# Turning by products in column groups, and loads, reciprocals and first value products moved by some slots, in a one-core attention and FFN layer

## The reference

```python
def _L0_attn_ref(x, Wq, Wk, Wv, Wo, bo):
    q = (x @ Wq).reshape(B, C, H, D).transpose(0, 2, 1, 3)   # k and v alike
    scores = jnp.einsum('bhqd,bhkd->bhqk', q, k)
    scores = jnp.where(causal, scores, -jnp.inf)
    attn = jax.nn.softmax(scores / jnp.sqrt(jnp.float32(E)), axis=-1)
    ctx = jnp.einsum('bhqk,bhkd->bhqd', attn, v)
    return ctx.transpose(0, 2, 1, 3).reshape(B, C, E) @ Wo + bo
...
def _L0_ffn_ref(x, weight, bias):
    xq, xs = _mx_quantize(x2)      # blocks of 32, nearest value of a 6-bit grid
    wq, ws = _mx_quantize(w2)
    return (xq * xs) @ (wq * ws).T + bias
...
x = x + _L0_attn_ref(_layernorm(x), ...)
x = x + _L0_ffn_ref(_layernorm(x), ...)
```

## Time and profile before

| what | value |
|---|---|
| median of 3 runs | 2030.56 us (2029.66 to 2031.16) |
| the profiled execution | 2027.43 us |
| its span, first to last instruction | 2025.7 us |
| mean granted TensorE clock | 0.978 of full speed |
| busy: PE, DVE, ACT, POOL | 93%, 84%, 66%, 40% |

### The profile page before, as it was taken

How to read it: one execution, slowest core, us unless ns; L and a number is a source line. 1 busy time by engine, 2 the same in 40 slices (tenths; PEclk the granted TensorE clock), 3 DMA queues, 4 the chain that set the end, 5 groups by cost and what they waited for, 6 DMA issues and landing times.

```text
span 2025.7 us, 72471 instructions
## 1 busy us (share of the span) xinstructions
PE 1878.4 (93%) x30309; PEld 823.9 (41%) x30309; DVE 1706.3 (84%) x4358; ACT 1342.0 (66%) x2817; POOL 811.1 (40%) x1123
## 2 busy tenths in 40 slices
PE   6799899898999999999999999999999999999994
PEld 2334344343344343534334344434443444444432
DVE  4798897878997979797898979797799899999975
ACT  5357666676776767676676766667666676777660
POOL 4323324231344545454243646444345444211232
PEclk9899999999999999999999999999999999999987
DMA  5442231413132251612414161340613221140000
GB/s 161 124 105 83 60 88 37 116 53 96 41 95 76 72 125 44 142 53 64 114 47 117 38 158 54 79 111 19 161 49 88 68 71 51 39 100 27 11 33 22
DMA packets 173349, 156.51 MB, mean 77 GB/s; under 512 B 43224, under 2 KB 160734, under 8 KB 173022
## 3 DMA queue, kind: packets, MB, share of 16 engines
q1 hardware_dynamic: 173020, 151.88, 27.9%
HBM read 91.89 MB, written 57.02 MB: 74 GB/s over the span
## 4 chain that ended last, share of the span: by engine, by line
PE 56%; DVE 27%; SPq 6%; issue 5%; ACT 3%; POOL 2%; DMA 2%; POOLq 0%; DVEq 0%; ACTq 0%
PE psum L1459 39%; PE psum L1500 15%; DVE max_parts L1202 12%; DVE psum L1197 7%; SPq L677 5%; ACT probs L1015 2%; DVE max_parts L1197 1%; PE psum L1527 1%; ACT acc_sb L1024 1%; PE psum L1519 1%; DVE block_max L1331 1%; DMA qk_scratch<-shop 1%; DVE out_shop L1354 1%; DVE out_shop L1362 1%; DVE stats L1290 1%
## 5 line engine op out<-in xcount | busy, mean ns | idle before, releaser
L1015 ACT ACTIVATE probs<-psum 128x512 f32<-128x512 f32 (+3 forms) x2560 | 1209.9, 538 | 461.3 <-PE psum L1459 448.1
L1202 DVE TENSOR_REDUCE max_parts<-psum 128x1 f32<-128x512 f32 x1536 | 960.1, 682 | 97.8 <-PE psum L1459 93.5
L1459 PE MATMUL psum<-k_rows,q_rows 96*32 96x512 bf16 (+3 forms) x10240 | 851.6, 352 | 65.2 <-DVE max_parts L1197 31.8
L1459 PE MATMUL psum<-q_rows,k_rows 99*32 99x512 bf16 (+3 forms) x10240 | 892.6, 351 | 9.2 <-DMA q_rows<-max_rows 3.9
L1500 PE MATMUL psum<-probs,v_in 128*17 128x512 f32 (+3 forms) x5120 | 591.3, 535 | 15.8 <-ACT acc_sb L1024 15.1
L1197 DVE CUSTOM_DVE_ANT_0 psum<-psum,causal 128x128 f32<-128x128 f32 (+3 forms) x1024 | 475.4, 518 | 97.6 <-PE psum L1459 93.7
L1459 PEld LDWEIGHTS psum<-k_rows,q_rows 96*32 96x32 bf16 x10240 | 280.0, 97 | 475.1 <-DVE max_parts L1202 162.8
L1459 PEld LDWEIGHTS psum<-q_rows,k_rows 99*32 99x32 bf16 x10240 | 282.9, 96 | 402.0 <-ACT probs L1015 209.7
L843 POOL TENSOR_SCALAR_AFFINE_SELECT probs<-probs 128x512 f32<-128x512 f32 x256 | 165.2, 645 | 652.2 <-ACT probs L1015 651.9
L1500 PEld LDWEIGHTS psum<-probs,v_in 128*17 128x17 f32 x5120 | 143.0, 98 | 111.4 <-issue 33.9
L1197 DVE DVE_READ_ACCUMULATOR2_ANT max_parts<- 128x1 f32 x1024 | 145.1, 142 | 0.0
(11 more groups left out here) (157 smaller groups left out, 1205.2 us busy)
## 6 DMA issues: line engine op xcount, KB each, us to landing
q_rows<-qk_scratch SPq DMA_DIRECT2D x384, 64.0 KB, 2.7
k_rows<-qk_scratch SPq DMA_DIRECT2D x384, 64.0 KB, 2.6
qk_scratch<-shop SPq DMA_DIRECT2D x56, 384.0 KB, 3.4
sums_scratch<-acc_sb SPq DMA_DIRECT2D x48, 256.0 KB, 2.3
shop<-in_L_attn_x SPq DMA_DIRECT2D x19, 512.0 KB, 4.4
v_scratch<-shop SPq DMA_DIRECT2D x16, 544.0 KB, 4.3
v_in<-v_scratch SPq DMA_DIRECT2D x64, 136.0 KB, 2.9
out_shop<-in_L_attn_x SPq DMA_DIRECT2D x12, 512.0 KB, 8.7
```

The lines of the kernel that those rows point to most:

```text
L1015: nc.scalar.activation(probs[s % NPROBS][:, h, a:CHUNK], bank[SCORE_BANKS[n % 3]][:, a:CHUNK], ACT.Exp, scale=SCALE).then_inc(probs_ready, 1)
L1202: nc.vector.tensor_reduce(max_parts[k % 2][:, first:first + heads, t % TILES, c], ring_bank(UNIT_USE[n])[:, 0:heads * width] .rearrange("p ...
L1459: ins = nc.tensor.matmul(out[r:r + COLUMNS], weights[:, r:r + COLUMNS], moving, start=start, stop=stop)
```

## The change

Four edits. The load of x of chunks 4 to 15 is placed at start - 6 in place of start - 2, four slots earlier in SP's order. `invert` is placed from p + 7 on in place of p + 5, two slots later, and by that the output work of a chunk behind it, by 2 to 7 slots for most. The turns are made by `by_columns`, as products of the block with the unit matrix: 16 products of 32 columns for four blocks, in place of 4 transposes of 128 columns (`turn_weights`, once, stays). And the first `values` of each row chunk stands after h = 3 in place of h = 1.

```diff
 def place_project(n, start):
-    sync(start - 2, "load_x", n)
+    sync(start - 6, "load_x", n)
...
-            p = vector(p + 5, 0.6, "invert", n) + 1
+            p = vector(p + 7, 0.6, "invert", n) + 1
...
             def turn_acc(k):
...
-                    ins = nc.tensor.transpose(ring_bank(use)[:, j * P:(j + 1) * P], acc_sb[k % 2][:, j * P:(j + 1) * P],
-                                              ident[:, :])
+                    ins = by_columns(ring_bank(use)[:, j * P:(j + 1) * P], acc_sb[k % 2][:, j * P:(j + 1) * P],
+                                     ident[:, :], True, True)
...
             def turn_x(n, e):
...
-                    ins = nc.tensor.transpose(ring_bank(use)[:, j * P:(j + 1) * P],
-                                              x_in[n % 2][:, j, e * P:(e + 1) * P], ident[:, :])
+                    ins = by_columns(ring_bank(use)[:, j * P:(j + 1) * P], x_in[n % 2][:, j, e * P:(e + 1) * P],
+                                     ident[:, :], True, True)
...
-                    if h == 1 and 0 <= p - 2 < NS:
+
+                    if 0 <= p - 2 < NS and h == (3 if p - 2 in FIRSTS else 1):
                         values(p - 2)
```

4 lines of the change are left out of this document (2 added, 2 removed).

## The result

The changed kernel is slower. Its median is 2045.62 us (2042.77 to 2048.05, 4 runs) beside 2030.11 us of the kernel before on the same chip, a ratio of 1.0078 with an interval of 1.0064 to 1.0091: +15.5 us, where the forecast was -6.1 and the range ended at 2038. The profiled execution took 2047.51 us with a span of 2045.8, 20.1 us over the 2025.7 of before.

What follows compares the result with a forecast made beforehand. TensorE, busy 93% of the span, was taken to bound the kernel. Stalls -18.3, clock -7.8, prologue +4.7, turns +19.3 and first values -4 gave -6.1 us: 2024.5 us, range 2012 to 2038.

Steps and rivals of the forecast that it cites:

- The four stalls: TensorE's stalls behind VectorE's loads of x and denominators go, -18.3 us, and their half-clock windows, -7.8 us.
- The prologue: Chunk 4's earlier load of x delays load_rows(0, 2), so PE stands longer in slot 0: +4.7 us.
- The turns: Turns as two-pass products, 0.109 us a pass: +15 us in the slots, +2.3 prologue, +2.0 tail, in all +19.3.
- rival of dear turns: Weight loads of the turn products don't hide, 0.138 us a pass: +18 us, 2042 us; chance 0.13.
- factor of four: Turn products lose the fast float32 transpose mode, 1.74 us for four blocks, some 2095 us; one part in a hundred within dear turns.
- The first failed step: Output work behind the later invert finds other free places, none in the tail: 0, with 3 us on both sides.
- the stalls move: Rival: something else late takes the place of the loads, half of the 26 us stays: +13, 2037 us; chance 0.12.
- the term of the first values: In slots with first values, the 15.1 us wait mostly returns as another: -4 us, ends -15 and +3.
- the reciprocals: invert two slots later removes three stalls at the denominators' loads, 13.0 - 0.5 us, and 5.3 us of half clock.
- the load of x: Four slots earlier, chunk 7's stall goes, 5.75 us and 2.5 us of half clock, against +4.7 us in the prologue.
- rival of cheap turns: VectorE's lag hides half the turns' cost, most of the values' 15.1 us wait goes: -19, 2011 us; chance 0.17.
- PE has no stall over 2 us between 130 and 1900 us: Sign of the forecast: after the change TensorE has no stall over 2 us in that stretch.

Runs made afterwards that it cites:

- hand_moves: Kernel before, load of x of chunk 7 and reciprocals with their loads for chunks 0, 4, 8 moved after planning: 2014.79 us beside 2029.36.
- units_behind: Kernel before with first values after the fourth score group and the units of h = 2 and 3 behind them: 2038.28 us beside 2030.67.
- values_only: Kernel before with only the first values of each row chunk after h = 3 in place of h = 1: 2037.51 us beside 2029.9.

## Why the forecast was wrong

**The four stalls (-18.3, clock -7.8)** were read rightly, in place, cause and size. All four went, with their windows at 1.2 GHz; in hand_moves the four places give 24.5 us together, against 26.1 of the sum.

**The prologue (+4.7)** was right for the edit alone. The wait for `k_rows` near 95 us was to grow from 0.7 to about 5; in the kernel with that edit alone it is 4.6 us near 98, and slot 20 is 4.7 us later. In the changed kernel slot 0 begins 3.7 us later than before already, and the wait is 2.3 us, until 100.17.

**The turns (+19.3)** were right in the price of a pass (0.109 us, from the earlier trace rows) and in the count. The term measured 15.2 us as a median and 18.4 between spans. The rival of dear turns, with 0.138 us a pass, is out. Its small chance for a factor of four can be settled too. Four blocks take 0.87 us as products and 0.59 as transposes up to the next group, so the factor here is 1.5; against 0.44 us, the 0.68 of the earlier trace rows without the 0.24 that go with the change of mode, it is 2. The Trainium skill, TensorE: Matmul & The Clock Gate, Terms, calls the transpose mode four times faster for float32; these products in column groups don't bear that out. The Trainium skill, TensorEngine Tiling (Array Packing), Key Properties, says that a change of the tiling mode drains the TensorE; the rows agree, with 0.24 us for a turn of four.

**The first failed step** is the sentence "The output work behind goes 2 to 7 slots later into other free places, and none of it into the tail: I take 0, with 3 us on both sides." In the kernel with that edit alone 6.3 and 10.1 us are lost at two places, some 5 and 10 of them by waits and half clock. What was missed is two steps off: the output work takes free places that projections had, the projections' store moves by three slots, and in SP's order it falls behind a block of twelve loads that takes 6.7 us to issue. GpSimd waits for that store, with a mask in its queue that TensorE needs. The forecast looked at SP's order at the prologue and at chunk 7, and not at the stores whose slots moved. The rival that came nearest is "the stalls move", 2037 us; it named another statistics step or the first store of the inverse, not this one. The edit gave 4.3 us where its terms say 17.8.

**The second failed step** is the term of the first values, -4. Its working was right for one chunk: the wait of 0.49 us becomes one of 0.3 to 0.5 for the fourth group, and the waits for the copy went. Those for exponentials grew by 7.8 us, half of what went, where the forecast had nearly all of it, so by waits the term was even too cautious. Its bounds of -15 and +3 were too narrow above. It took the slot by itself, from the last unit to the slot's end, and left out what comes to lie beside the wait: with the waits for VectorE near it, five more windows of 3.4 us at 1.2 GHz, 8.5 us. In units_behind, with 22.6 us of waits for exponentials and 84 us at 1.2 GHz, less than before, the same late place costs as much by waits alone; that ScalarE is handed its work less evenly is the reading of both, not a thing measured by itself. The edit cost 7.6 us in place of giving 4.

Together, with the medians of the single edits in place of their terms: -6.1 + 13.5 for the reciprocals (-4.3 for -17.8) + 0.9 for the load of x (-2.7 for -3.6, prologue included) + 11.6 for the values - 4.1 for the turns = +15.8, against +15.5 measured. In the rival of cheap turns "10 us less for each" does not fit its own sum, which takes 7.3 and 6 us off; its 2011 us follow from the sum.

**The forecast's signs.** "PE has no stall over 2 us between 130 and 1900 us" was the one that showed the first failure at once; the lines for the denominators, the clock behind the old stalls and the pass came true. VectorE waits for x only in the prologue, 3.3 us, where it waited 3.1 before the change; the wait for `k_rows` is 2.3 us in place of 5, and the new waits for `probs` are half of those that went. A list of signs can be true in the main while the time is wrong by 20 us.

## What to carry to other kernels

When an edit goes through a planner, list every entry whose slot changes, the loads and stores above all, and follow each into the in-order queue that holds it: the cost of a move is what ends up behind something long there. An edit of the finished plan, entry by entry, gave 14.6 us where a like set of moves through the planner gave 6.0, and showed in the same run that the reading of the stalls had been right.

To take away a wait for another engine, look first at where the awaited instruction stands in that engine's queue: one place earlier for one copy gave 9.6 us, where putting the waiting work later cost 7.6. By the reading above, which fits three kernels and was not tried alone, the work put later was also what spaced out the supply of that other engine.

## What the runs showed of the hardware

A loss of TensorE's clock does not need a long stall. In the kernel with the first values late, a wait of 0.20 and one of 1.12 us within 2 us were followed by 3.4 us at a granted clock of 0.54, and in the kernels here 68 to 105 us of a span are spent at 1.2 GHz. Nor does more waiting in small pieces always bring it: units_behind has 22.6 us of waits for exponentials, values_only 9.7, and the first spends 84 us at 1.2 GHz, the second 105. So two kernels with the same waits in sum can be 9 us apart in busy time, with the same instructions (1878.4 and 1887.8 us). The kernel before itself spread over 2023 to 2036 us in 27 runs, so a difference under 5 us can't be read from a few runs.

Products of four column groups with the unit matrix start 0.22 us after the group ahead (810.21 to 810.43 in the changed kernel), where a transpose starts 0.31 after it: the edit did save what goes with the change of mode. That saving, 0.24 us for a turn of four with the 0.09 ahead of it, is smaller than the 0.44 us of the second pass that it is bought with.
